# A spectral tokenizer and five blocks on one core: the preparation in another order

## The reference, cut to what matters

```python
h = layer_norm(x @ fc0_w + fc0_b, ln0_g, ln0_b)          # embedding: 3 -> 32 channels
for i in range(4):
    x1 = irfft2(einsum('bixy,ioxy->boxy', rfft2(h)[12x12 modes, both ends], w1r[i] + 1j*w1i[i], w2r.. ))
    x2 = einsum('bchw,oc->bohw', h, conv_w[i]) + conv_b[i]   # the 1x1 weights
    h = layer_norm(x1 + x2, ln_g[i], ln_b[i]);  if i < 3: h = gelu(h)
h = fc3(gelu(fc2(gelu(fc1(h)))))
```

## Time and profile before

| | us |
|---|---|
| median of 3 runs | 4682.74 (4681.69 to 4684.64) |
| the profiled execution | 4677.02 |
| its span | 4675.2 |
| PE busy | 3900.5 (83%) |
| DVE, ACT, POOL busy | 2320.5, 2091.3, 809.9 |
| SP's 64 stores: KB each, median from issue to landing | 288.0, 4.7 |

### The profile page before, as it was taken

One profiled execution on the slowest core, in us unless ns is written; L12 is line 12 of the kernel. 1 busy time (PEld: TensorE's weight loads), 2 busy tenths in 40 slices (PEclk: granted clock), 3 DMA queues, 4 the chain that ended last, 5 costly groups with the idle time before them and its releaser, 6 DMA issues. The chain is left out here.

```text
span 4675.2 us, 102193 instructions
## 1 busy us (share of the span) xinstructions
PE 3900.5 (83%) x39344; PEld 2983.1 (64%) x39344; DVE 2320.5 (50%) x5028; ACT 2091.3 (45%) x3178; POOL 809.9 (17%) x540
## 2 busy tenths in 40 slices
PE   0089999998899999979999999799999995686168
PEld 0058888852788888337888873478888724572056
DVE  6564454532545445234544551354454503968756
ACT  1154454456545444664544547554454481230012
POOL 0031131220213112111311320122122300001020
PEclk9989999999999999989999999899999997688679
DMA  8501111110022020100211201021120001000000
GB/s 203 179 25 63 43 62 63 42 55 4 22 75 70 22 83 22 56 3 22 83 63 39 66 22 56 3 75 30 64 82 22 22 2 32 1 1 0 0 1 10
DMA packets 168551, 208.67 MB, mean 45 GB/s; under 512 B 156386, under 2 KB 158663, under 8 KB 159858
## 3 DMA queue, kind: packets, MB, share of 16 engines
q1 hardware_dynamic: 166370, 178.13, 13.3%
q10 hardware_dynamic: 1680, 23.60, 2.0%
HBM read 142.57 MB, written 59.12 MB: 43 GB/s over the span
## 5 line engine op out<-in xcount | busy, mean ns | idle before, releaser
L767 POOL TENSOR_TENSOR rstd<-var,mhalf 128x16 f32<-128x16 f32 x240 | 698.9, 2912 | 38.9 <-POOL var L764 17.6
L744 ACT ACTIVATE h<-tp,gb 128x512 f32<-128x512 f32 x640 | 554.1, 869 | 277.2 <-PE tp L465 275.4
L708 DVE TENSOR_REDUCE ssum<-sq 128x16 f32<-128x512 f32 x640 | 432.2, 682 | 300.7 <-ACT sq L732 298.0
L764 POOL TENSOR_TENSOR var<-ssum,eps 128x16 f32<-128x16 f32 x240 | 52.4, 218 | 2942.2 <-DVE ssum L708 2942.2
L465 PE MATMUL tp<-ident,xn 128*128 128x128 f32 x2560 | 418.2, 289 | 104.2 <-DVE xn L699 86.2
L457 PEld LDWEIGHTS main<-convw,h 128*128 128x128 f32 x3072 | 378.5, 196 | 150.4 <-issue 150.4
L506 PE MATMUL main<-fwd_w,pix 128*128 128x96 f32 x4096 | 464.8, 276 | 7.0 <-ACT pix L598 7.0
L506 PEld LDWEIGHTS main<-fwd_w,pix 128*128 128x128 f32 x4096 | 459.8, 192 | 10.3 <-DVE pix L598 8.6
L732 ACT ACTIVATE sq<-main 128x512 f32<-128x512 f32 x480 | 287.5, 602 | 346.2 <-PE main L457 238.4
L465 PEld LDWEIGHTS tp<-ident,xn 128*128 128x128 f32 x2560 | 304.0, 147 | 198.3 <-DVE xn L699 170.9
L424 PE MATMUL aux<-inv_r,yd 96*48 96x64 f32 x8192 | 421.1, 257 | 6.9 <-DVE zq L598 3.3
(11 more groups left out here) (240 smaller groups left out, 5944.6 us busy)
## 6 DMA issues: line engine op xcount, KB each, us to landing
mixw<-mix_scratch SPq DMA_DIRECT2D x15, 4608.0 KB, 14.8
y_scratch<-t_w SPq DMA_DIRECT2D x256, 144.0 KB
yd<-y_scratch SPq DMA_DIRECT2D x32, 1152.0 KB, 7.1
mix_scratch<-mixw SPq DMA_DIRECT2D x64, 288.0 KB, 4.7
mixw<-mix_scratch ACTq DMA_DIRECT2D x1, 4608.0 KB, 13.7
h<-in_L_tok_w1r ACTq DMA_DIRECT2D x6, 576.0 KB, 9.7
h<-in_L_tok_w1i ACTq DMA_DIRECT2D x6, 576.0 KB, 10.1
h<-in_L_tok_w2r ACTq DMA_DIRECT2D x6, 576.0 KB, 18.4
```

The costliest lines, as they stand in the source:

```text
L708: dve.tensor_reduce(ssum[:, c % 4, :], sq[:, c % 2, :].rearrange("p (n c) -> p n c", c=CH), AX.X, ALU.add).then_inc(red_done, 1)
L744: act.activation(out, in_, fn, bias=gb[:, 1, stage:stage + 1] if l is None else gb[:, 1, bass.ds(stage, 1)], scale=gb[:, 0, stage:stage + ...
L767: pool.tensor_tensor(rstd[:, c % 4, :], var[:, c % 4, :], mhalf[:, :], ALU.pow).then_inc(rstd_done, 2)
```

## The change

Nothing is computed in another way. In the first block:

- DVE does the small parts (bias, embedding weights, 1x1 weights) ahead of the four layers, so its wait for all 68 small loads now stands ahead of layer 0.
- SP issues, behind the small loads and ahead of all stores of `mixw`, the 16 image loads of the first group, then the store of the embedding weights, waits for its landing, and issues both loads of them.
- POOL zeroes `xs` when PE's small matmuls are done. DVE's memset and the semaphore `xs_zero` are gone.
- In the second block SP no longer loads the first images, and the first block no longer ends with a wait for the embedding weights' store.

```diff
 @block.sync
                 for dst, src in loads:
                     sp.dma_start(dst, src).then_inc(p_small, 16)
+                for u in range(UNITS):
+                    sp_images(sp, 0, u)
+                sp.wait_ge(p_done, 3)
+                sp.dma_start(embw_scratch, embw_of(0)).then_inc(p_bstore, 16)
+                sp.wait_ge(p_bstore, 16)
+                for u in range(UNITS):
+                    sp.dma_start(embw_of(u), embw_scratch).then_inc(x_in[u], 16)
                 for n in range(LAYERS):
...
-                sp.wait_ge(p_done, 3)
-                sp.dma_start(embw_scratch, embw_of(0)).then_inc(p_bstore, 16)
-                sp.wait_ge(p_bstore, 16)
 @block.vector
+                dve.wait_ge(p_small, 16 * N_SMALL)
...
                 for n in range(LAYERS):
                     dve.wait_ge(p_raw[n % 2], 128 * (n // 2 + 1))
...
-                dve.wait_ge(p_small, 16 * N_SMALL)
...
+            @block.gpsimd
+            def _(pool):
+                pool.wait_ge(p_pe, 2)
+                pool.memset(xs[:, :], 0.0)
 # second block
-                dve.memset(xs[:, :], 0.0).then_inc(xs_zero, 1)
-                dve.wait_ge(xs_zero, 1)
-                act.wait_ge(xs_zero, 1)
-                for u in range(UNITS):
-                    sp_x(sp, 0, u)
```

More of the change, by code:

```diff
@@ L206, in tokenizer, with sp_images @@
         mask = sq[0:97, 1, 0:32]
+        x_in = [sem(f"x_in{u}") for u in range(UNITS)]
+        def sp_images(sp, g, u):
+            for b in range(NB):
+                for a in range(NA):
+                    img = g * GROUP + (u * UIMG + b * NA + a)
+                    sp.dma_start(xb_of(u)[b:128:2, :].rearrange("r (k a n) -> r a k n", k=8, a=NA)[:, a],
+                                 t["x"][bass.ds(img, 1)].rearrange("a r (k w) c -> r (a k) (w c)", k=8)).then_inc(x_in[u], 16)
         with nc.Block() as block:
@@ L261, in _ @@
                     dve.memset(yd[96:97, u * YC + 1024:u * YC + 2048], 1.0)
[L262 to L278, removed]
                 dve.wait_ge(p_small, 16 * N_SMALL)
@@ L299, in _ @@
                                         aux[1][32 * a:32 * a + 32, 32 * l:32 * l + 32])
+                for n in range(LAYERS):
+                    dve.wait_ge(p_raw[n % 2], 128 * (n // 2 + 1))
+                    for v in range(2):
+                        dve.tensor_reduce(rsum[:, 2 * (n % 2) + v, :], raw[n % 2][v].rearrange("p (o n) -> p n o", o=CH), AX.X,
+                                          ALU.add).then_inc(p_sum, 1)
+                    dve.wait_ge(p_sum, 2 * (n + 1))
+                    for k in range(4):
+                        if n >= 1:
+                            dve.wait_ge(p_store[k], 64 * n)
+                        for v in range(2):
+                            dve.scalar_tensor_tensor(
+                                out=cent[:, k, :, :, v, :],
+                                in0=rsum[:, 2 * (n % 2) + v, :].rearrange("p (x y k) -> p x y k", x=M1, k=4)[:, :, :, k].unsqueeze(3).to_broadcast([128, M1, KQ, CH]),
+                                scalar=-1.0 / CH,
+                                in1=raw[n % 2][v].rearrange("p (o x y k) -> p x y o k", o=CH, x=M1, k=4)[:, :, :, :, k],
+                                op0=ALU.mult, op1=ALU.add).then_inc(p_cent, 1)
             @block.scalar
@@ L344, in tokenizer @@
         turn_full, turn_free = (sem(n) for n in ("turn_full", "turn_free"))
-        mixw_in, xs_zero, y_ready, y_stored = (sem(n) for n in ("mixw_in", "xs_zero", "y_ready", "y_stored"))
-        x_in = [sem(f"x_in{u}") for u in range(UNITS)]
+        mixw_in, y_ready, y_stored = (sem(n) for n in ("mixw_in", "y_ready", "y_stored"))
         yd_in = [sem(f"yd_in{u}") for u in range(UNITS)]
@@ L792, in sp_x @@
         def sp_x(sp, g, u):
[L793 to L797, removed]
+            sp_images(sp, g, u)
             sp.dma_start(embw_of(u), embw_scratch).then_inc(x_in[u], 16)
```

## The result

| | before | changed |
|---|---|---|
| median, us | 4681.69 (4679.58 to 4684.64, 5 runs) | 4702.18 (4696.99 to 4712.14, 5 runs) |
| the profiled execution / its span | 4677.02 / 4675.2 | 4702.01 / 4700.2 |
| PE's first image matmul | 233.31 | 250.70 |

The ratio is 1.0048, 95% interval 1.0034 to 1.0063: slower by 20.5 us (interval 16 to 29), inside the forecast of 4686 to 4719 and 4 us from its 4706. PE's start moved by 17.4 us of these.

A forecast was written before the change was run, and what follows sets the result against it. The prediction held that only PE's first image matmul, at 233.31 us, could move: 49.6 us won, 72.7 lost at layer 1's first STT, so 23 us slower than the 4682.7 median, 4706; range 4686 to 4719.

The forecast's parts named there:

- PE's start carries the time: Whole kernel: the change can only move PE's first image matmul, at 233.31 us; the same instructions follow in the same order.
- Small loads through at 73.6, landed at 75.5, DVE free for layer 0 at 81.6: Preparation: SP's small loads end at 73.6 instead of 82.45; DVE waits for them, then does small parts for 6.1 us.
- Images by 0.72: SP's queue in the preparation: 16 image loads at 0.72 us each go out from 73.6 to 85.1.
- 97 rows on one engine, both loads on the same, in order, in turn with the raw loads: DMA ahead of layer 0's stores: 194 rows at 0.165 us hold layer 1's first STT until 163.4, was 90.70.
- From there to DVE's end as before, 81.4: DVE from layer 1's first STT to its end: unchanged 81.4 us, so DVE ends at 244.8.
- Tail 11.6: From DVE's end to PE's start: 11.6 us, ACT's `mixw` issue and table load coming last; PE starts at 256.4.
- main term: PE's start: 49.6 us won against 72.7 lost, so 23 us slower.
- A: Layer 1: 97-row transfers don't hold up the stores; PE starts at 222.1, 11 us faster, 4671; chance 0.07.
- B: Layer 1: shorter hold, two engines (+7) or raw loads taking no turns (+1); 4683 to 4690; chance 0.12.
- C: SP's queue: longer hold, small loads stay late or images go out slowly; one +32, both +41, 4714 to 4724; chance 0.13.

The follow-up runs named there:

- e6: Kernel before the change, order unchanged, with the embedding weights' store and all its loads cut into 96 rows and 1 row; 4655.7 us, ratio 0.9943.
- e1: Changed kernel with the preparation's store and two loads of the 97-row embedding weights cut into 96 rows and 1; 4670.4 us, ratio 0.9977 to before.
- e2: Changed kernel with the 97-row embedding loads moved, unit 0's behind layer 2's stores, unit 1's into the second block; 4667.3 us, ratio 0.9971 to before.
- e3: Changed kernel with only unit 1's embedding load moved into the second block, unit 0's left ahead of the stores; 4683.7 us.
- e7: Kernel before the change with DVE zeroing the spectrum twelve times instead of once, to delay PE's start; 4705.4 us, ratio 1.0049.
- e4: Changed kernel with SP's order put back as before, DVE's order and POOL's memset kept as changed; 4719.7 us, ratio 1.0092 to before.
- e9: Kernel with small parts in layer 1, images and cut embedding transfers behind layer 2's stores, POOL's memset, plus the 97-row mask load cut; 4640.7 us.

## Why the prediction was right

- *PE's start carries the time.* Right. Over ten kernels (the changed one and nine experiments) whose start lies between -47.0 and +37.7 us from before, the median differs from it by -1.6 to +5.3 us.
- *Small loads through at 73.6, landed at 75.5, DVE free for layer 0 at 81.6.* Measured 73.61, 75.28, 81.57. The argument, that nine slow issues were slow only beside layer 2's raw loads, holds.
- *Images by 0.72.* 0.69. The slower row (18.96 for eight) would have misled by some 25 us; it stood behind the 97 rows, and e6 shows 5.26 without them.
- *97 rows on one engine, both loads on the same, in order, in turn with the raw loads.* Each leg is shown: e1 and e6 (shape), e2 (place), e3 and the packets (one behind the other; turns). The STT started at 160.1, predicted 163.4. The term was 3.3 us too large, with errors on both sides: the loads were issued at 102.5 and not at 104.3, a row took 0.16 us and not 0.165, and beside the raw loads 24 rows went in 24 us where one row per raw piece had given 16; on the other side one engine's raw pieces ended near 142 and not 139. What the prediction had only as the stores' share waiting on one engine was also, and for longer, SP unable to issue them (29 us for the second store).
- *From there to DVE's end as before, 81.4.* Measured 79.6. Here the size was off: the old 81.4 held a second wait for stores, 1.77 us before the last two STTs of layer 2, that didn't come back. Why not is open; it is 0.47 in e7, whose preparation is that of before.
- *Tail 11.6.* 11.0. ACT's `mixw` issue and table load were the last to come, as said.
- Together these put PE's start at 256.4, measured 250.7. The forecast of the time was nearer (4706 to 4702) than its own main term (+23 to +17.4). That is luck: the median took 3 us more behind the start than before's did, which no term of the sum had. All versions but e7 show 1 to 5 us of this kind. For the profiled execution the larger part is PE's longer busy time in the last stretch; why it leans to one side isn't settled.
- *Rivals.* A (no hold) and B (two engines, or no turns) fall with the idle of 31.24 us and e3. C didn't come: small loads through at 73.61, images out in 11.04. What e1 and e4 add: the loss ahead of DVE's end is two losses, 37 us from DVE's wait and 31 from the hold, and only the first comes with the new order as such.

## What to carry to other kernels

Moving loads ahead to hide them moves them ahead of something in the same queue: ask for each what stands behind it, who waits for that, and how many DMA engines it uses. A transfer of 97 rows in the trace shows as a DMA share of 0.06; cut into 96 and 1 rows it took 2.5 us instead of 17, and that edit alone gained 26 us where the reordering lost 20. An engine's preparation is best put where its timeline shows idle time (here 17 us on DVE, 14 on SP), not at the front, where it waits for its inputs.

## What the runs showed of the hardware

- Queue entries that used one engine delayed the later entries of their queue, which have a share on that engine: behind two loads of 97 rows DVE waited 31.24 us for four stores, and 0 once the loads were cut (e1) or moved (e2).
- SP's issues stood still behind such entries, and the time shows up as a long issue of an innocent DMA (36.63 us of a 384-byte load before, 44.28 us for eight stores after; the first is gone in e9 and the second in e1, where the entries ahead are cut). I take it that one engine's part of the queue was full; how much it holds was not measured.
- Two queues took turns about piece by piece although the sizes were far apart: 85 pieces of 36 KB and 72 of 96 bytes in the same 7 us, and in the changed kernel 24 rows of 4 KB in 24 us beside raw pieces of 18 KB, against 56 in 9 us alone. Small loads beside large ones on the other queue therefore crawl (e9).
- POOL's memset of 128x4704 f32 took 4.02 us, DVE's 3.98.
